# Expert rows added into one sum in DRAM by adding scatters, in a Macaron layer on one core

## The chip, the cores and the metric

The kernel runs on one core of one Trainium2 chip. The metric is the device time of one execution in microseconds (us); lower is better. TensorE (PE) multiplies matrices, VectorE (DVE) and ScalarE (ACT) work element by element and move results out of the matrix buffers (PSUM banks), GpSimd (POOL) does some element work and issues the indirect DMAs, and SyncE (SP) issues the plain ones.

## The reference

```python
x = L0_attn_inputs                                   # 4 x 256 tokens of 256, float32
x = x + 0.5 * ffn(layernorm(x))                      # mixture of experts
x = x + attention(layernorm(x))                      # 16 heads of 16, causal
x = x + 0.5 * ffn(layernorm(x))

def ffn(layer_input):
    logits = x @ router_weight.T                     # 8 experts
    top_vals, top_idx = jax.lax.top_k(logits, 2)
    gates = softmax(top_vals)
    for each expert e:                               # w_in 1024 x 256, w_out 256 x 512
        a, b = split(x @ w_in[e].T)
        acc = acc + gates[:, e] * (silu(a) * b @ w_out[e].T)
    return acc + bias
```

Each of the 1024 tokens takes part in two experts, so there are 2048 pairs of a token and an expert.

## The kernel before

**Blocks.** An expert phase (`ffn(0)` before the attention, `ffn(1)` behind it) is routed first: VectorE finds the two experts of each token, TensorE counts ranks by products, and the pairs, sorted by expert, are laid out in `BLOCKS` = 23 blocks of 128 slots. A block holds one expert's pairs; slots left over are empty. A one-hot product (L1264) finds which pair stands in each slot, and with it come `gather_row` and `scatter_row`.

**The loop over blocks.** For block j POOL gathers 128 normalised rows from `xn_scratch` (`gather`, L502). TensorE turns them (`turn_block`), multiplies them by both halves of w_in (`project`, three products for each since the float32 operands are split into a high and a low part), turns the gated middle (`turn_gated`) and multiplies by w_out (`combine`, L1311, again in three parts). In TensorE's order `combine(j)` stands between the turning and the projection of block j + 2. ScalarE makes the high parts, `silu` and the copy of the result out of PSUM (`copy_y`, L670); VectorE makes the low parts: `xT_lo`, `g`, `wo_lo` and `gT_lo`. In the first phase both also split each w_in (`split_high`, `split_low`) three blocks ahead. The first blocks are written out, the middle ones run in a hardware loop. The order of each engine is the order of the code; semaphores tie them together.

**Where the rows go.** For the first `SCATTERED` = 21 blocks `copy_y` writes ungated rows to one of two buffers `y`, and POOL scatters them (L510) to `y_scratch`, at the row of their pair, so no two scatters meet. At the phase's end SyncE waits for all scatters and loads both rows of each token (eight loads of 256 KB, L433). They are gated and added by VectorE (`add_rows`, L1010) or gated by ScalarE (`scale_rows`) and added up by TensorE through identity products (`add_scaled`, L1342). The rows of the last `LAST` = 2 blocks never leave the core: they are gated with `slot_gate` and spread over the tokens by one-hot products (`spread`, L1324) into four accumulators, one for each pair of token tiles; `settle` (L1022) adds an accumulator to x. Their gates are written to DRAM and gathered slot by slot (`gather_gates`, L526), and `zero_rows` (L516) scatters zeros to the pairs' places in `y_scratch`. The bias is added to x by POOL (`add_bias`, L496) after block 6. TensorE runs warming products on ones (`warm`) where it would stand still.

## Time and profile before

| | |
|---|---|
| Three runs | 436.99, 437.62, 437.9 us; median 437.62 us |
| Profiled execution | 439.45 us, its span from the first to the last instruction 437.4 us |
| Mean granted TensorE clock | 0.977 of full speed |
| Busy: PE, DVE, ACT, POOL | 408.1, 300.9, 256.8, 247.3 us |
| Scatters (L512) | 42, POOL busy 60.2 us |
| Gathers (L506) | 46, POOL busy 50.4 us |
| Loads of the scattered rows | 16 of 256 KB, landing 5.0 us after issue (median) |
| DMA traffic | 38.90 MB, 89 GB/s over the span |

"Busy" is the time in which an engine executes; the rest of the span it waits. A wait matters only where something on the way to the end waits with it; that way is what the chain of waits shows. Landing is counted from the start of the instruction that issues a DMA to the DMA's semaphore. The first expert phase lies at about 5 to 156 us of the span, the attention behind it, the second expert phase from about 295 us to the end.

### The profile page before, as it was taken

Reading aid. Unit: us, or ns where it says so; the run is one execution under the profiler, and the core shown is the slowest. Engines: PE = TensorE matmul, PEld = TensorE weight load, DVE = VectorE, ACT = ScalarE, POOL = GpSimd, SP = SyncE. Lnnn points to the kernel's source line nnn. Section 1 sums busy time; section 2 is a strip of 40 time slices with the busy share of each in tenths; the row PEclk is TensorE's granted clock in tenths of the full one; section 3 lists DMA queues with packets and bytes.
Section 4 is the critical chain, followed back from the end, with each engine's and each line's share of the span. In section 5 each row is a group of like instructions: output and inputs, shape, how many; then the busy total and the mean of one; then the engine's idle time right before and its main releaser. Section 6 shows DMA issues by size and latency. Waiting matters only on the chain.

```text
span 437.4 us, 10190 instructions
## 1 busy us (share of the span) xinstructions
PE 408.1 (93%) x2918; PEld 332.6 (76%) x2919; DVE 300.9 (69%) x613; ACT 256.8 (59%) x638; POOL 247.3 (57%) x307
## 2 busy tenths in 40 slices
PE   7878999999999989799999999898799999999995
PEld 3546888888888857588888888674488888888884
DVE  6768996865566697787677676866366575556565
ACT  2706885556655454788788787622255555655552
POOL 5136446866468359567777577200365586754860
PEclk9689999999999999999999999987999999999999
DMA  8729961111211620000000000007451112112136
GB/s 284 247 51 381 390 214 49 49 48 60 60 48 36 213 89 0 2 1 2 2 1 0 0 0 0 1 1 258 155 178 54 57 37 72 60 48 52 44 91 220
DMA packets 25738, 38.90 MB, mean 89 GB/s; under 512 B 3056, under 2 KB 20720, under 8 KB 25712
## 3 DMA queue, kind: packets, MB, share of 16 engines
q1 hardware_dynamic: 19088, 24.41, 16.3%
q0 software_dynamic: 4544, 12.07, 9.2%
q10 hardware_dynamic: 2080, 2.10, 1.4%
q8 instruction: 14, 0.23, 0.2%
q14 instruction: 12, 0.10, 0.1%
HBM read 29.37 MB, written 9.19 MB: 88 GB/s over the span
## 4 chain that ended last, share of the span: by engine, by line
PE 66%; DVE 13%; DMA 9%; issue 4%; ACT 3%; POOL 2%; SPq 1%; DVEq 0%; ACTq 0%; POOLq 0%
PE bank L1298 23%; PE bank L1320 12%; PE bank L1456 6%; PE bank L1221 4%; PE bank L1467 4%; PE bank L1308 3%; DMA w_out<-in_wout_t 3%; DMA w_out<-y_scratch 3%; PE bank L1423 2%; PE bank L1274 2%; PE bank L1503 2%; DMA arena<-xn_scratch,gather_row 1%; DMA y_scratch<-arena,scatter_row 1%; DVE arena L859 1%; PE bank L1457 1%
## 5 line engine op out<-in xcount | busy, mean ns | idle before, releaser
L506 POOL DMA_INDIRECT arena<-xn_scratch,gather_row x46 | 50.4, 1096 | 72.1 <-PE bank L1274 41.9
L512 POOL DMA_INDIRECT y_scratch<-arena,scatter_row x42 | 60.2, 1434 | 34.2 <-ACT arena L678 31.2
L987 DVE TENSOR_TENSOR wo_lo<-w_out,wo_hi 128x1024 fp32r<-128x1024 f32 x46 | 60.8, 1322 | 4.1 <-PE bank L1320 1.8
L1298 PE MATMUL bank<-w_hi,xT_hi 128*128 x184 | 62.4, 421 | 1.2 <-ACT xT_hi L637 1.2
L992 DVE TENSOR_TENSOR gT_lo<-bank,gT_hi 128x512 fp32r<-128x512 f32 x46 | 31.7, 690 | 39.3 <-ACT gT_hi L652 39.2
L1298 PE MATMUL bank<-w_hi,xT_lo 128*128 x184 | 58.0, 396 | 0.0
L1298 PE MATMUL bank<-w_lo,xT_hi 128*128 x184 | 57.6, 394 | 0.0
L590 POOL TENSOR_TENSOR k_head<-k_hi,head_mask 128x256 fp32r<-128x256 f32 x64 | 38.7, 625 | 28.1 <-PE bank L1457 21.0
L645 ACT ACTIVATE arena<-bank 128x512 f32<-128x512 f32 x46 | 27.5, 598 | 46.1 <-PE bank L1298 46.1
L667 ACT ACTIVATE wo_hi<-w_out 128x1024 fp32r x46 | 48.8, 1061 | 6.5 <-issue 4.1
L976 DVE TENSOR_TENSOR xT_lo<-bank,xT_hi 128x256 fp32r<-128x256 f32 x46 | 19.5, 424 | 37.3 <-ACT xT_hi L637 37.1
L1456 PE MATMUL bank<-k_head,xT_hi 128*128 128x256 f32 (+1 forms) x128 | 39.8, 392 | 1.9 <-ACT probs L775 1.2
L1298 PEld LDWEIGHTS bank<-w_lo,xT_hi 128*128 128x128 f32 x184 | 34.8, 189 | 8.2
L1298 PEld LDWEIGHTS bank<-w_hi,xT_lo 128*128 128x128 f32 x184 | 34.8, 189 | 8.0
L590 POOL TENSOR_TENSOR k_head<-k_lo,head_mask 128x256 fp32r<-128x256 f32 x64 | 38.3, 618 | 0.6 <-DVE k_lo L1102 0.6
L678 ACT ACTIVATE arena<-bank 128x256 f32<-128x256 f32 x42 | 16.2, 385 | 36.5 <-PE bank L1320 36.5
L1221 PE MATMUL bank<-ones 128*128 128x512 f16 x102 | 33.2, 480 | 2.8 <-POOL ident L459 1.8
L767 ACT ACTIVATE probs<-bank,neg_max 128x256 f32<-128x256 f32 x64 | 29.9, 478 | 8.7 <-DVE neg_max L1115 8.6
L1320 PE MATMUL bank<-wo_hi,gT_hi 128*128 128x256 f32 x184 | 33.0, 301 | 1.4 <-ACT gT_hi L652 1.4
L785 ACT ACTIVATE pT_hi<-bank 128x384 f16<-128x384 f32 x64 | 28.0, 488 | 10.4 <-PE bank L1467 9.9
L1128 DVE SCALAR_TENSOR_TENSOR pT_lo<-bank,pT_hi 128x384 f16<-128x384 f32 x64 | 32.4, 548 | 0.6
L1001 DVE TENSOR_TENSOR arena<-arena,bank 128x512 f32<-128x512 f32 x46 | 31.2, 678 | 0.9 <-issue 0.9
(180 smaller groups left out, 966.5 us busy)
## 6 DMA issues: line engine op xcount, KB each, us to landing
w_raw<-in_win_t SPq DMA_DIRECT2D x8, 1024.0 KB, 10.7
w_out<-in_wout_t SPq DMA_DIRECT2D x16, 512.0 KB, 8.3
w_out<-y_scratch SPq DMA_DIRECT2D x16, 256.0 KB, 5.0
xn_scratch<-arena ACTq DMA_DIRECT2D x2, 1024.0 KB, 6.3
x<-in_x SPq DMA_DIRECT2D x4, 256.0 KB, 3.5
out<-x SPq DMA_DIRECT2D x4, 256.0 KB, 2.1
arena<-xn_scratch,gather_row POOLq DMA_INDIRECT x46, 3.5
y_scratch<-arena,scatter_row POOLq DMA_INDIRECT x46, 3.0
```

The source lines that it names most:

```text
L506: pool.indirect_dma_start(out=xb[j % 2][:, :], out_offset=None, in_=xn_dram, in_offset=bass.IndirectOffsetOnAxis(ap=gather_row[:, j:j + 1] ...
L512: pool.indirect_dma_start(out=y_dram, in_=y[j % 2][:, :], in_offset=None, out_offset=bass.IndirectOffsetOnAxis(ap=scatter_row[:, j:j + 1], ...
L590: ins = pool.tensor_tensor(k_head[s % KSLOTS][:, part, hh, :], k[:, c, :].bitcast(F32), head_mask[:, h % HPC:h % HPC + 1].to_broadcast([P, ...
L667: act.activation(wo_hi[u][:, :, :], w_out[:, bass.ds(e, 1), :, :].rearrange("p o c d -> p (o c) d"), ACT.Copy)\
L987: dve.tensor_tensor(wo_lo[:, :, :], w_out[:, bass.ds(e, 1), :, :].rearrange("p o c d -> p (o c) d"), wo_hi[u][:, :, :].bitcast(F32), ALU.s ...
L992: dve.tensor_tensor(gT_lo[:, :, :], bank[4][:, :].rearrange("p (c t) -> p c t", c=HK), gT_hi[:, :, :].bitcast(F32), ALU.subtract).then_inc ...
L1001: dve.tensor_tensor(g[:, :], sa[:, :], bank[2 + u][:, :], ALU.mult).then_inc(g_done, 1)
L1128: dve.scalar_tensor_tensor(pT_lo[u][:, :, :], bank[3 + hh][:, 0:3 * P].rearrange("p (k t) -> p k t", k=3), P_SCALE, pT_hi[u][:, :, :], ALU ...
L1221: pe.matmul(bank[into][:, :], ones[:, :], bc(ones[:, :], 1, [P, 512 // P, P]), start=True, stop=True)
L1298: last = pe.matmul(bank[2 * half + u][:, :], tok[u][:, k, :], wts[:, bass.ds(e, 1), k, half * H:(half + 1) * H], start=(part == 0 and k == ...
L1320: last = pe.matmul(bank[y_bank(j)][:, 0:D], tok[:, c, :], wts[:, c, :], start=(part == 0 and c == 0), stop=(part == 2 and c == HK - 1))
L1456: pe.matmul(to, q[:, 1 if tail else 0, :], keys[:, part, :, 0:width], start=(n == 0), stop=False)
```

## The change

The scattered rows are gated first (`copy_y` scales by a column of `slot_gate`, now with a gate for each slot of all 23 blocks) and are scattered with an adding DMA into `sum_scratch`, one row for each token. The sum starts as a copy of x, written by SyncE (`start_sums`); at the end it is loaded straight into x, four loads of 256 KB. Two pairs of one token meet in one row, so each scatter waits for the one before it. Empty slots go to 128 spare rows behind the sum. The gates per slot come out of one-hot products: POOL computes the gates and splits them into three bf16 parts (`split_gates`), VectorE multiplies the block one-hots by them, TensorE multiplies 16 times by the row one-hots (69 columns), and VectorE sums the three parts. The bias enters the accumulators by a product of ones with a tile whose first three rows hold its three bf16 parts (`split_bias`, `spread_bias`). The zero scatters, the gates' way through DRAM, the additions of rows and the addition of the bias on POOL are gone. One w_in and one w_out are loaded before the first gathers rather than behind them, SyncE waits between the loads, and 11 rather than 18 warming products stand before the first phase's pair products.

```diff
-WARM_START, WARM_RANKS, WARM_PLAN, WARM_TURNED = 12, (18, 18), (6, 6), (4, 4)
+WARM_START, WARM_RANKS, WARM_PLAN, WARM_TURNED = 12, (11, 18), (6, 6), (4, 4)
@@ sync
+            def start_sums(f, first, tiles):
+                some = slice(first, first + tiles)
+                sp.dma_start(sum_rows[:, some, :], x[:, some, :]).then_inc(sum_started, 16)
-            load_w_in(0)
-            load_w_in(1)
-            load_w_in(2)
+            for e in range(EARLY):
+                load_w_in(e)
             load_w_out(0)
+            load_w_out(1)
+            load_w_in(EARLY)
             for parity in range(2):
                 sp.wait_ge(gathered[parity], 16)
-            for e in range(EARLY, E):
+            start_sums(0, 0, TILES)
+            load_w_out(2)
+            for e in range(EARLY + 1, E):
                 load_w_in(e)
-                load_w_out(e - EARLY + 1)
-            for e in range(E - EARLY + 1, E):
-                load_w_out(e)
+                load_w_out(e - 1)
+                sp.wait_ge(win_loaded[e - 1], 16)
+            load_w_out(E - 1)
...
+                    for b in range(BATCH):
+                        sp.wait_ge(attn_added, b + 2)
+                        start_sums(1, 2 * b, 2)
...
                 for i in range(TPAIRS):
-                    for k in range(TOPK):
-                        sp.dma_start(y_in[:, 2 * i:2 * i + 2, k, :], y_rows[:, k, 2 * i:2 * i + 2, :])\
-                            .then_inc(y_loaded[i], 16)
+                    sp.dma_start(x[:, 2 * i:2 * i + 2, :], sum_rows[:, 2 * i:2 * i + 2, :]).then_inc(y_loaded[i], 16)
@@ gpsimd
             def scatter(f, j):
                 pool.wait_ge(y_copied, f * SCATTERED + j + 1)
-                pool.indirect_dma_start(out=y_dram, in_=y[j % 2][:, :], in_offset=None,
-                                        out_offset=bass.IndirectOffsetOnAxis(ap=scatter_row[:, j:j + 1], axis=0))\
-                    .then_inc(scattered[j % 2], 16)
+                if j:
+                    pool.wait_ge(scattered[(j - 1) % 2], 16 * ((S_EVEN, S_ODD)[(j - 1) % 2] * f + (j + 1) // 2))
+                else:
+                    pool.wait_ge(scatter_ready, f + 1)
+                    pool.wait_ge(sum_started, 16 * (1 + BATCH * f))
+                pool.indirect_dma_start(out=sum_dram, in_=y[j % 2][:, :], in_offset=None,
+                                        out_offset=bass.IndirectOffsetOnAxis(ap=scatter_row[:, j:j + 1], axis=0),
+                                        compute_op=ALU.add).then_inc(scattered[j % 2], 16)
+            def split_gates(f):
+                ...
+                pool.wait_ge(e1_ready, f + 1)
+                then_gate(pool.tensor_scalar(den[:, :], e1[:, :], 1.0, None, ALU.add))
+                then_gate(pool.tensor_tensor(den[:, :], den[:, :], half_ones[:, 1, :], ALU.pow))
+                ...
@@ scalar
+                if isinstance(j, int) and j == 0:
+                    act.wait_ge(slot_gate_ready, f + 1)
+                column = slot_gate[:, j:j + 1] if isinstance(j, int) else slot_gate[:, bass.ds(j, 1)]
+                act.activation(y[u][:, :], bank[6][:, 0:D], ACT.Copy, scale=column).then_inc(y_copied, 1)
@@ vector
+            def mark_gates(f):
+                dve.wait_ge(gate_parts_ready, f + 1)
+                for part in range(PARTS):
+                    ins = dve.tensor_tensor(blk_gate[:, :, part, :], blk_hot[:, :, :],
+                                            bc(gate_part[:, part, :], 2, [P, PAIRS, BLOCKS]), ALU.mult)
+                ins.then_inc(gates_hot, 1)
+            def gather_gates(f):
+                dve.wait_ge(gates_done, f + 1)
+                parts = bank[7][:, 0:PARTS * BLOCKS].rearrange("p (a j) -> p j a", a=PARTS)
+                dve.tensor_reduce(slot_gate[:, :], parts, AX_X, ALU.add).then_inc(slot_gate_ready, 1)
@@ tensor
+            def spread_bias():
+                pe.wait_ge(bias_ready, 1)
+                for i in range(TPAIRS):
+                    pe.matmul(bank[ACC_BANK[i]][:, :], ones[:, :], bc(bias_rows[:, :], 1, [P, 2, D]), start=True, stop=False,
+                              skip_group_check=True)
...
+                    if not gated_next:
+                        spread_bias()
+                        spread(f, j - 1, range(1))
                     combine(f, j, u)
...
-                for j in range(SCATTERED, BLOCKS):
-                    spread(f, j)
-                add_scaled(f)
+                spread(f, SCATTERED, range(1, TPAIRS))
+                spread(f, SCATTERED + 1)
```

TensorE's order at the end of the second phase, from block 21's output product on, before (L1308 turns the gated middle, L1320 is the output product, L1334 the one-hot products):

```order
L1320 MATMUL bank<-wo_hi,gT_hi 128x256 x4
L1320 MATMUL bank<-wo_lo,gT_hi 128x256 x4
L1320 MATMUL bank<-wo_hi,gT_lo 128x256 x4
L1308 MATMUL bank<-ident,arena 128x128 x4
L1320 MATMUL bank<-wo_hi,gT_hi 128x256 x4
L1320 MATMUL bank<-wo_lo,gT_hi 128x256 x4
L1320 MATMUL bank<-wo_hi,gT_lo 128x256 x4
L1334 MATMUL bank<-gated_before,slot_hot 128x256 x16
L1334 MATMUL bank<-gated_last,slot_hot 128x256 x16
```

and after (L1319 is the output product, L1334 now the bias product, L1347 the one-hot products):

```order
L1319 MATMUL bank<-wo_hi,gT_hi 128x256 x4
L1319 MATMUL bank<-wo_lo,gT_hi 128x256 x4
L1319 MATMUL bank<-wo_hi,gT_lo 128x256 x4
L1307 MATMUL bank<-ident,arena 128x128 x4
L1334 MATMUL bank<-bias_rows,ones 128x512 x4
L1347 MATMUL bank<-gated_before,slot_hot 128x256 x4
L1319 MATMUL bank<-wo_hi,gT_hi 128x256 x4
L1319 MATMUL bank<-wo_lo,gT_hi 128x256 x4
L1319 MATMUL bank<-wo_hi,gT_lo 128x256 x4
L1347 MATMUL bank<-gated_before,slot_hot 128x256 x12
L1347 MATMUL bank<-gated_last,slot_hot 128x256 x16
```

The bias products and four of block 21's one-hot products now stand ahead of the last output product.

VectorE's order at the same place, before (L992 is gT_lo, L987 wo_lo, L1007 `gate_y_low`, L1018 `add_rows`, L1029 `settle`):

```order
L980 TENSOR_LOAD block_expert
L980 ISA x2
L992 TENSOR_TENSOR gT_lo<-bank,gT_hi 128x512
L1001 TENSOR_TENSOR arena<-arena,bank 128x512
L987 ISA
L987 TENSOR_TENSOR wo_lo<-w_out,wo_hi 128x1024
L992 TENSOR_TENSOR gT_lo<-bank,gT_hi 128x512
L1007 SCALAR_TENSOR_TENSOR gated_before<-bank,slot_gate,gated_before 128x256
L1018 SCALAR_TENSOR_TENSOR x<-w_out,gate,x 128x256 x2
L1007 SCALAR_TENSOR_TENSOR gated_last<-bank,slot_gate,gated_last 128x256
L1018 SCALAR_TENSOR_TENSOR x<-w_out,gate,x 128x256 x4
L1029 TENSOR_TENSOR x<-x,bank 128x512
```

and after (L1007 is now gT_lo, L1002 wo_lo, L1022 `gate_y_low`, L1030 `settle`):

```order
L995 TENSOR_LOAD block_expert
L995 ISA x2
L1007 TENSOR_TENSOR gT_lo<-bank,gT_hi 128x512
L1016 TENSOR_TENSOR arena<-arena,bank 128x512
L1002 ISA
L1002 TENSOR_TENSOR wo_lo<-w_out,wo_hi 128x1024
L1022 SCALAR_TENSOR_TENSOR gated_before<-bank,slot_gate,gated_before 128x256
L1007 TENSOR_TENSOR gT_lo<-bank,gT_hi 128x512
L1022 SCALAR_TENSOR_TENSOR gated_last<-bank,slot_gate,gated_last 128x256
L1030 TENSOR_TENSOR x<-x,bank 128x512 x4
```

`gate_y_low` of block 21 has moved ahead of gT_lo of block 22, and only the settlings are left behind the two.

VectorE's order at the first phase's first blocks, before (L873 splits w_in, L976 is xT_lo, L980 reads a block's expert, L1001 is g):

```order
L873 TENSOR_TENSOR w_lo<-w_raw,w_hi 128x1024 x2
L976 TENSOR_TENSOR xT_lo<-bank,xT_hi 128x256
L873 TENSOR_TENSOR w_lo<-w_raw,w_hi 128x1024 x2
L976 TENSOR_TENSOR xT_lo<-bank,xT_hi 128x256
L980 TENSOR_LOAD block_expert
L980 ISA x2
L1001 TENSOR_TENSOR arena<-arena,bank 128x512
L987 ISA
L987 TENSOR_TENSOR wo_lo<-w_out,wo_hi 128x1024
L873 TENSOR_TENSOR w_lo<-w_raw,w_hi 128x1024 x2
L980 TENSOR_LOAD block_expert
```

and after (L886 splits w_in, L991 is xT_lo, L977 `mark_gates`, L985 `gather_gates`):

```order
L886 TENSOR_TENSOR w_lo<-w_raw,w_hi 128x1024 x2
L991 TENSOR_TENSOR xT_lo<-bank,xT_hi 128x256
L886 TENSOR_TENSOR w_lo<-w_raw,w_hi 128x1024 x2
L991 TENSOR_TENSOR xT_lo<-bank,xT_hi 128x256
L977 TENSOR_TENSOR arena<-arena,gate_part 128x16x23 x3
L995 TENSOR_LOAD block_expert
L995 ISA x2
L1016 TENSOR_TENSOR arena<-arena,bank 128x512
L985 TENSOR_REDUCE slot_gate<-bank 128x23
L1002 ISA
L1002 TENSOR_TENSOR wo_lo<-w_out,wo_hi 128x1024
L886 TENSOR_TENSOR w_lo<-w_raw,w_hi 128x1024 x2
```

Three multiplications have come in ahead of the first g, and a reduction behind it.

## Rows read from the trace of the kernel before

**Rows 1.** Page, part 4: the chain that ended last, shares of the span by engine.

```profile
PE 66%; DVE 13%; DMA 9%; issue 4%; ACT 3%; POOL 2%; SPq 1%; DVEq 0%; ACTq 0%; POOLq 0%
```

**Rows 2.** Chain of waits, second phase's end: start us, us, what.

```profile
407.22 1.44 PE bank L1320 x12
...
412.08 1.45 PE bank L1320 x12
...
419.16 3.01 DMA y_scratch<-arena,scatter_row
...
425.71 6.16 DMA w_out<-y_scratch
...
434.12 0.69 DVE x L1029
```

**Rows 3.** Timeline, second phase's end: start, us, engine, line, operation, count [idle before <-releaser].

```profile
423.23 1.22 DVE L987 TENSOR_TENSOR wo_lo<-w_out,wo_hi 128x1024 fp32r<-128x1024 f32 x1 [0.92 <-PE bank L1320]
...
424.14 0.74 PE L1320 MATMUL bank<-wo_hi,gT_hi 128*128 128x256 f32 x4 [0.69 <-ACT gT_hi L652]
...
425.69 2.08 PE L1334 MATMUL bank<-gated_before,slot_hot 128*128 128x256 f32 x16
...
426.48 0.48 DVE L1007 SCALAR_TENSOR_TENSOR gated_last<-bank,slot_gate,gated_last 128x256 fp32r<-128x256 f32 x1
...
427.60 2.08 PE L1334 MATMUL bank<-gated_last,slot_hot 128*128 128x256 f32 x16
```

**Rows 4.** Timeline, first phase's end.

```profile
148.14 2.08 PE L1334 MATMUL bank<-gated_before,slot_hot 128*128 128x256 f32 x16
...
152.24 0.68 DVE L1029 TENSOR_TENSOR x<-x,bank 128x512 f32<-128x512 f32 x1
...
153.62 0.86 DVE L1018 SCALAR_TENSOR_TENSOR x<-w_out,gate,x 128x256 f32<-128x256 f32 x2
...
154.40 0.68 DVE L1029 TENSOR_TENSOR x<-x,bank 128x512 f32<-128x512 f32 x1
```

**Rows 5.** One line's instructions: scatters, all; scatter of 47.0; gathers of 321 to 409.

```profile
L512 POOL DMA_INDIRECT y_scratch<-arena,scatter_row x42: 980/1524/1968, 41.9 to 419.2; - x42
...
DMA to landing us min/median/max: 2.4/3.0/6.8
...
DMA to landing us min/median/max: 6.8/6.8/6.8
...
DMA to landing us min/median/max: 2.7/3.3/3.8
```

**Rows 6.** First phase's routing: chain row of the warming products, then VectorE's timeline.

```profile
16.74 6.43 PE bank L1221 x18
...
21.69 0.54 DVE L943 TENSOR_TENSOR arena<-arena,pair_id 128x368 f16<-128x368 f32 x1
...
23.60 0.18 DVE L952 TENSOR_SCALAR pair_i<-bank 128x23 int32<-128x23 f32 x1 [0.90 <-PE bank L1264]
```

**Rows 7.** VectorE's timeline, first blocks of the first phase.

```profile
34.29 0.42 DVE L976 TENSOR_TENSOR xT_lo<-bank,xT_hi 128x256 fp32r<-128x256 f32 x1 [2.79 <-ACT xT_hi L637]
35.29 0.69 DVE L1001 TENSOR_TENSOR arena<-arena,bank 128x512 f32<-128x512 f32 x1 [0.57 <-issue]
...
42.23 2.35 DVE L873 TENSOR_TENSOR w_lo<-w_raw,w_hi 128x1024 fp32r<-128x1024 f32 x2
44.51 0.68 DVE L992 TENSOR_TENSOR gT_lo<-bank,gT_hi 128x512 fp32r<-128x512 f32 x1
```

**Rows 8.** Timeline around POOL's addition of the bias in the first phase.

```profile
75.32 4.63 POOL L500 TENSOR_TENSOR x<-x,bias_half 128x2048 f32<-128x2048 f32 x1
...
77.04 3.99 DVE L987 TENSOR_TENSOR wo_lo<-w_out,wo_hi 128x1024 fp32r<-128x1024 f32 x1
...
76.18 0.64 PE L1320 MATMUL bank<-wo_hi,gT_lo 128*128 128x256 f32 x4
...
81.69 0.74 PE L1320 MATMUL bank<-wo_hi,gT_lo 128*128 128x256 f32 x4
```

More of the change, by code:

```diff
@@ L41 @@
 ACC_BANK = (7, 5, 3, 2)
[L43 to L44 removed]
 PAIRS = TOPK * TILES
 NEG = -1.0e30
+PARTS = 3
 AHEAD = 4
@@ L966, in route @@
[L966 to L970 removed]
+                then(dve.tensor_scalar(empty[:, :], pair_of, 0.0, trash_id[:, 0:1], ALU.is_equal, ALU.mult))
```

205 lines of the change are left out of this document (84 added, 121 removed).

## Prediction

> **What bounds the kernel now.** I read the page's chain by engine first, then the whole chain of waits in order of time, then the timeline of the two ends of the expert phases and of the start of the first, and last the landing times of the indirect DMAs. Two thirds of the chain are TensorE's own matmuls [rows 1]. In both expert phases the steady stage is TensorE's alone: the last product of one block starts 4.86 us after that of the block before (407.22, 412.08) [rows 2]. Whatever is done to scatters, bias or gates inside that stage is worth nothing as long as it fits into 4.87 us. The chain leaves TensorE at the stage's end: scatter 20 (3.01 us), eight loads of the scattered rows one after the other on SyncE, the last landing 6.16 us after its issue, and a last addition on VectorE at 434.12, which ends at 434.81; 2.6 us later the span ends [rows 2]. TensorE itself is through with the last one-hot products at 427.60 + 2.08 = 429.7 [rows 3], so some 5 us of the end are the way of the rows through DRAM. The first phase ends in the same way, but there VectorE's own work is the chain, with one addition of scattered rows (0.86 us) between two settlings [rows 4].
>
> **The end of the second phase.** After the change half the bytes are read back (four loads of 256 KB, straight into x), and the additions on VectorE, the scalings on ScalarE and the identity products on TensorE are gone. The last scatter starts at 419.2 as before; with 3.0 us of landing the four loads are issued from 422.2 on, each about 0.47 us, and should all be there by 427.5. What is late next is TensorE. The order there is new: bias product, block 21's products for pair 0, and only then the last block's output product. Pair 0's products need gate_y_low(21), which now stands right behind split_out_low(22) on VectorE: 423.23 + 1.22 = 424.45, + 0.48 = 424.9 [rows 3]. Four products at 1.91 / 16 = 0.12 us (the two groups of 16 start 1.91 us apart) end at 425.4; the last output product, which started at 424.14, starts 1.3 us later and, with 1.55 us as before (424.14 to 425.69), ends at 427.0. Then twelve products (1.43 us) and sixteen (1.91 us) give 430.35, and 0.1 for the handover, 430.5. The gating of block 22 (VectorE was through with it at 426.96, 1.3 us after the last output product) is hidden by the twelve. The four bias products stand in the wait for gate_y_low(21) and cost nothing; if that wait were gone, they would cost some 0.9 us. The settlings of pairs 0 to 2 lie under the products of the later pairs, the last one takes 0.69: 431.2 in place of 434.8. **-3.6 us.**
>
> **The end of the first phase** has the same pattern 277.55 us earlier (425.69 against 148.14). Pair 0 is complete there at 428.95 - 277.55 = 151.4 in place of 152.24, and the addition of 0.86 us between the first and the second settling goes, so that the second starts at about 152.75 in place of 154.40 [rows 4]. From there the chain is unchanged VectorE work. **-1.6 us.**
>
> **The adding scatter.** Each scatter now waits until the one before it has landed, and behind that wait on POOL stands the gather for the block five further on. Before, a scatter landed 2.4 to 3.0 us after its issue in the quiet stages, 0.98 to 1.6 us of which is POOL's own instruction; a gather landed after 2.7 to 3.8 [rows 5]. An adding scatter has to read its rows first, which no row shows. Bounds: 2.4 (as a plain one) and 3.0 + 2.6 = 5.6 (a whole gather's journey, its median 3.3 less about 0.7 of overlap, in series). I take 3.8, nearer to the scatter, since source and target rows can be read side by side. Under 4.8 it costs nothing in the steady stage. At the two ends a later landing is hidden too: pair 0 is needed at 428.95, so that the last scatter may take some 6.5 us. While the weights load, though, the scatter of 47.0 landed after 6.8 us [rows 5], more than a block (5.3 us there, below). With the new waits the first three or four scatters fall behind by 1.5 to 2 us each; gathers still come before TensorE needs them by my count, with little over. I put 0.4 us for it (0 to 5).
>
> *The Trainium skill* (DMA: Bandwidth & Descriptors, "Latency and other measured facts") gives 0.2 us on average for an access to HBM and 2 us under high load. Added to the plain scatter that is 3.2 or 5.0 us; by the second figure the steady stage would be slowed, by the first not. No row here decides between them.
>
> **The start of the first phase.** The one-hot pair products wait behind 18 warming matmuls that end at 23.17, while their operand is ready at 21.69 + 0.54 = 22.23 [rows 6]. With 11 of them (6.43 x 11 / 18 = 3.93 us from 16.74) TensorE is free at 20.7; the pair products then start at 22.3 and pair_i at about 22.85 in place of 23.60 (before it VectorE is busy till 22.7). **-0.75 us**, if the clock's dip behind it is no deeper than now. Against it stands the new gate work on VectorE: three multiplications of 128x368, each as the pair one (0.54, [rows 6]), between copy_xT_low(1) (ends 34.71) and the first g (35.29, [rows 7]): 1.62 us, of which the 0.58 us in which VectorE waits for its register load hide some; then a wait for 16 products on TensorE and a reduction, 0.2 to 0.3. For the next blocks VectorE is without a pause, since it splits the weights beside its usual work: 0.42 for xT_lo, 0.69 for g, 1.22 for wo_lo, 2.35 for w_lo and 0.68 for gT_lo are 5.3 us a block [rows 3, 7]. So it all arrives: **+1.3 us.** The loads are reordered, with 1.5 MB (one w_in, one w_out) brought forward and 1 MB of the residual written in between; as VectorE and not a load sets this stage, I count 0. The eight small gate steps on POOL run before the plan is there.
>
> **The bias.** The addition of the bias to all of x on POOL (4.63 us) held wo_lo on VectorE for 3.99 us in place of 1.22, and TensorE's third part of the output product came 5.51 us after the last one (76.18, 81.69) in place of 4.87 [rows 8]. It goes in both phases; in the second it cost nothing. **-0.6 us.** Its replacement, ten operations of 128x256 over three blocks in the first phase, fits between scatter and gather.
>
> **The second phase's start.** The 16 products of 69 columns for the gates stand on TensorE between block 1's halves, where little is waited for: at the price of those with 23 columns (23.17 to 23.60 with the handover, [rows 6]) or a bit over, +0.5. The gate multiplications on VectorE fall beside the first gather's descriptors, and the gate steps on POOL beside VectorE's routing, in which every step is on the path: +0.6 for both (0 to 2).
>
> The last price rests on [rows 8]: VectorE stood still for a POOL instruction. *The Trainium skill* (SBUF — State Buffer, "Who interferes with whom") says that a VectorE instruction with two SBUF inputs and a GpSimd one that reads SBUF exclude each other for the whole instruction. The trace agrees. By that rule a gate multiplication could hold the first gather for its 0.54 us and POOL's steps the routing for some 0.7 us in each phase, 1.9 us in place of my 0.6: 435.2.
>
> **Sum:** -3.6 - 1.6 + 0.4 - 0.75 + 1.3 - 0.6 + 0.5 + 0.6 = -3.75 us. The profiled execution had a span of 437.4 and took 439.45; it would take 435.7. The median of the runs is 437.62, 1.83 below it, so the forecast is 433.9.
>
> **Rivals.**
> *The chain of adds sets the pace (slower).* If an adding scatter lands later than about 4.8 us after its issue, each of some 20 scatters in a phase follows the last at landing + 0.1, and copy_y and through it TensorE wait for y. At 5.4, between the two bounds and near the upper, that is 0.63 x 20 x 2 = 25 us, less some 3 us at each end that the loads have to spare: 437.6 - 3.75 + 19 = 453. For it: the upper bound of [rows 5]; against it: 1.9 us between a plain scatter and the block's length.
> *It falls behind only while the weights load.* The scatters of the first four blocks land after 7 to 8.5 us, copy_y(3) waits, and 2 to 3 us are lost once: 436.0. For it: 6.8 us in [rows 5].
> *The hidden steps are not hidden (no change).* POOL's gate steps hold the routing twice for 1 to 1.5 us, the 1.62 us of multiplications hold the first gather, and the gate products start late: +3.5, 437.4. For it: [rows 8]; against: tiles of 8 and 16 columns.
> *More from the loads.* If, against my reading, loads brought forward shorten the first eight blocks by 0.3 us each, 2.4 us together: 431.5. Against it: VectorE's 5.3 us of such a block by themselves [rows 7].
>
> **How the numbers follow.** Forecast 0.52 (432.5 to 435.2), adds set the pace 0.18, behind under the loads 0.15, nothing hidden 0.07, more from the loads 0.08. A measurement here tells 0.2%, 0.9 us, from no change. Faster: 0.52 + 0.15 + 0.08 = 0.75; within it 0.07; slower 0.18. The range leaves out the most of the slower case and a sliver below: 430.8 to 441.0.
>
> **What would show it.** In the new profile: scatters landing under 4.8 us in the quiet stages and a POOL that waits for y_copied and not for scattered; blocks 4.87 us apart; the last output product starting 1.3 us later against its block's cadence; the last settling released by TensorE and not by a DMA, some 3.6 us earlier; pair_i at 22.8; the first g delayed. The forecast is wrong if the block period of the steady stage is above 4.9 us, or if the loads of x release the last settlings.

## The result: 7 to 8 us slower, and the profile after

The changed kernel takes 445.71 us (median of 4 runs, 444.52 to 445.9), the kernel before 437.76 beside it: a ratio over all runs of 1.0152, 95% interval 1.0121 to 1.0184. (The two medians lie 8.0 us apart, the ratio stands for 6.7 us.) The forecast was 433.9 us with a range to 441.0, so it had the wrong sign. The profiled execution took 445.52 us with a span of 443.8 (before 439.45 and 437.4), at granted clocks of 0.969 and 0.977. The two spans differ by 6.4 us; that is what the readings below divide up.

First the chain by engine and by line (part 4 of the page of after):

```profile
PE 53%; DMA 21%; DVE 11%; POOL 6%; issue 4%; ACT 4%; DVEq 0%; ACTq 0%; POOLq 0%
PE bank L1297 17%; DMA sum_scratch<-arena,scatter_row 15%; PE bank L1319 9%; PE bank L1461 6%; PE bank L1472 4%; DMA xn_scratch<-arena 3%; DMA arena<-xn_scratch,gather_row 3%; PE bank L1428 2%; PE bank L1220 2%; PE bank L1307 2%; PE bank L1508 2%; POOL sum_scratch L525 2%; ACT arena L694 2%; PE bank L1273 1%; PE bank L1462 1%
```

TensorE's share has gone from 66% [rows 1] to 53%, and the adding scatters hold 15%, where the plain ones had 1% of the chain before. To find where the time went I took the start of each block's output product (L1320 before, L1319 after) and subtracted. What a block "takes" is, below, the time from the start of the output product before it to that of its own.

| stretch (start of the output product of block ...) | before | after | added |
|---|---|---|---|
| first phase, 0 | 38.05 | 40.28 | +2.23 |
| 0 to 8 | 41.96 | 42.85 | +0.9 |
| 8 to 9 (bias addition gone) | 5.60 | 4.86 | -0.7 |
| 11 to 14 | 14.59 | 19.86 | +5.3 |
| 19 to 22 | 12.30 | 17.88 | +5.6 |
| 22 to the second phase's 0 | 172.77 | 168.17 | -4.6 |
| second phase, 0 to 21 | 102.07 | 102.07 | 0 |
| 21 to 22 | 2.71 | 4.48 | +1.8 |
| 22 to the end of the span | 13.2 | 9.2 | -4.0 |

So some 11 us are lost in two places of the first phase. The stretch 19 to 22 has three parts: 2.2 us at block 20, 1.6 at block 21, and 1.8 at block 22, which is the new order (the second phase's 21 to 22 has the same 1.8). The second phase's steady stage lost nothing: 4.87 us a block, as said. It has the same chain of adding scatters and the same one-hot rows on POOL at its end, but its first scatters land after 4.4 and 4.0 us and there is no bias to split; its blocks 19 and 20 take 4.86.

**How the first scatters go.** Chain of waits of after (start us, us, what):

```profile
44.24 9.05 DMA sum_scratch<-arena,scatter_row
...
53.34 0.73 issue
54.06 6.56 DMA sum_scratch<-arena,scatter_row
...
61.39 4.25 DMA sum_scratch<-arena,scatter_row
...
66.40 3.91 DMA sum_scratch<-arena,scatter_row
```

While weights load, two adding scatters land after 9.05 and 6.56 us, where a plain one of that stage had 6.8 [rows 5]. After that, from 75 us to the first phase's end, the landings are these (line L525 of after):

```profile
DMA to landing us min/median/max: 3.8/3.9/4.5
```

(The view is of 75 to 155 us.) The next scatter starts 0.77 us after a landing (44.24 + 9.05 = 53.29, and 54.06; I had 0.1). At its shortest the chain's period is 4.65 us (scatters 12 to 14, 115.81, 120.47 and 125.11), against a block of 4.87. But it doesn't work the backlog off at 0.2 us a block. Scatter 0 starts 4.0 us after its block's output product (44.24 against 40.28), scatter 2 9.6 us after it. In the loading stage, whose blocks are longer, that falls to 7.4 us at scatter 6, and there it stays: 7.6 at scatter 9 (95.57 against 87.99), 7.5 at 14, 7.6 at 17. From 6 to 9 and from 14 to 17 the scatters are 4.9 us apart, the same as the blocks, with landings of 3.9 to 4.5. The landing goes with the gather behind it on POOL: where that starts 1.9 us after the scatter, the landing is 3.75 to 3.9; where it starts 2.2 us after it or more, mostly 4.0 to 4.4. A gather waits for TensorE, so a chain that gets ahead meets longer landings. That this is what holds the backlog fits these times but was not tested.

**What the backlog does.** POOL's timeline of after, where the bias is made into rows:

```profile
95.57 1.87 POOL L525 DMA_INDIRECT sum_scratch<-arena,scatter_row  x1 [1.71 <-ACT arena L694]
96.92 1.46 POOL L555 TENSOR_SCALAR bias_half<-bias_half 128x256 f32<-128x256 f32 x1
98.45 0.40 POOL L557 CAST arena<-bias_half 128x256 bf16<-128x256 f32 x1
98.93 0.68 POOL L559 TENSOR_TENSOR arena<-bias_half,arena 128x256 f32<-128x256 f32 x1
99.69 1.64 POOL L561 TENSOR_TENSOR bias_rows<-arena,ident 128x256 bf16<-128x256 bf16 x1
101.60 1.05 POOL L513 DMA_INDIRECT arena<-xn_scratch,gather_row  x1 [0.27 <-POOL bias_rows L561]
102.95 1.62 POOL L525 DMA_INDIRECT sum_scratch<-arena,scatter_row  x1 [0.31 <-issue]
```

and TensorE's of the same time:

```profile
104.49 0.44 PE L1273 MATMUL bank<-ident,arena 128*128 128x128 f32 x2 [1.86 <-DMA arena<-xn_scratch,gather_row]
104.69 0.71 PE L1319 MATMUL bank<-wo_hi,gT_hi 128*128 128x256 f32 x4
```

The gather at 101.60 is block 14's, and TensorE turns block 14 ahead of block 12's output product. Since scatter 9 came at 95.57, four bias operations (with the scatter's own instruction they last from 95.57 to 101.33) push that gather beyond the need: TensorE stands for 1.86 us. It happens for three bias parts running (blocks 12, 13 and 14). The same happens at the end, where the one-hot rows for the last two blocks stand between scatter and gather:

```profile
139.82 1.82 POOL L525 DMA_INDIRECT sum_scratch<-arena,scatter_row  x1 [1.73 <-ACT arena L694]
141.12 2.91 POOL L574 TENSOR_SCALAR slot_hot<-col,slot_token 128x128 fp32r<-128x128 f32 x4
144.20 1.80 POOL L513 DMA_INDIRECT arena<-xn_scratch,gather_row  x1 [0.17 <-issue]
```

That gather is block 22's; it lands 4.55 us later, and block 20's output product waits for it until 148.98. What follows is the clock (TensorE's timeline, then a stretch of it with its granted clock behind the busy times):

```profile
148.79 0.44 PE L1273 MATMUL bank<-ident,arena 128*128 128x128 f32 x2 [1.96 <-DMA arena<-xn_scratch,gather_row]
149.50:153.00 3.50, 3.50 (x15) 3.12 (x14) 2.31 (x3) 0.62 (x2) 2.78 (x4) 0.53 0.03 5
```

After standing for 1.96 us TensorE is granted 0.53 of full speed (the lower of its two levels, 1.2 GHz, for nearly all of the stretch), and block 21 takes 6.28 us. In the profiles of *old order* and *gates early* below, block 20 waits as long (6.93 and 6.98), the clock stays whole, and block 21 takes 4.73. So the 1.6 us of block 21 are the clock's, and come or not after the same wait.

**The second phase's end** (timeline of after):

```profile
431.93 1.03 PE L1334 MATMUL bank<-bias_rows,ones 128*128 128x512 bf16 x4
...
433.52 1.90 SPq L439 DMA_DIRECT2D x<-sum_scratch  x4
...
433.98 0.72 PE L1347 MATMUL bank<-gated_before,slot_hot 128*128 128x256 f32 x4 [1.03 <-DVE gated_before L1022]
...
434.53 0.64 PE L1319 MATMUL bank<-wo_hi,gT_hi 128*128 128x256 f32 x4
...
437.41 2.08 PE L1347 MATMUL bank<-gated_last,slot_hot 128*128 128x256 f32 x16
...
438.19 2.48 DVE L1030 TENSOR_TENSOR x<-x,bank 128x512 f32<-128x512 f32 x4 [1.03 <-PE bank L1347]
```

It is the order that was forecast: bias products hidden in the wait, the last output product late, the loads of x done in time, the last settlings released by TensorE and not by a DMA as in [rows 2, 3].

### The profile page after: what moved, and what is told of

The parts are those of the page before. It is cut to its first block, busy times and chain, and to the rows that moved or that the text cites. A ratio compares the mean times of both kernels' runs of the same rounds, so it can differ in the third digit from the quotient of the medians.

```text
span 443.8 us, 10232 instructions
## 1 busy us (share of the span) xinstructions
PE 406.0 (91%) x2923; PEld 330.9 (75%) x2924; DVE 291.5 (66%) x587; ACT 255.3 (58%) x624; POOL 260.7 (59%) x321
## 3 DMA queue, kind: packets, MB, share of 16 engines
q0 software_dynamic: 8256, 11.54, 16.4%
## 4 chain that ended last, share of the span: by engine, by line
PE 53%; DMA 21%; DVE 11%; POOL 6%; issue 4%; ACT 4%; DVEq 0%; ACTq 0%; POOLq 0%
PE bank L1297 17%; DMA sum_scratch<-arena,scatter_row 15%; PE bank L1319 9%; PE bank L1461 6%; PE bank L1472 4%; DMA xn_scratch<-arena 3%; DMA arena<-xn_scratch,gather_row 3%; PE bank L1428 2%; PE bank L1220 2%; PE bank L1307 2%; PE bank L1508 2%; POOL sum_scratch L525 2%; ACT arena L694 2%; PE bank L1273 1%; PE bank L1462 1%
## 5 line engine op out<-in xcount | busy, mean ns | idle before, releaser
L525 POOL DMA_INDIRECT sum_scratch<-arena,scatter_row x42 | 74.9, 1784 | 59.6 <-ACT arena L694 44.8
L1297 PE MATMUL bank<-w_hi,xT_hi 128*128 x184 | 63.5, 427 | 1.3 <-ACT xT_hi L650 1.2
L1002 DVE TENSOR_TENSOR wo_lo<-w_out,wo_hi 128x1024 fp32r<-128x1024 f32 x46 | 57.4, 1247 | 5.4 <-PE bank L1319 4.0
L1007 DVE TENSOR_TENSOR gT_lo<-bank,gT_hi 128x512 fp32r<-128x512 f32 x46 | 31.7, 689 | 43.4 <-ACT gT_hi L665 43.4
L1297 PE MATMUL bank<-w_hi,xT_lo 128*128 x184 | 58.9, 402 | 0.0
L991 DVE TENSOR_TENSOR xT_lo<-bank,xT_hi 128x256 fp32r<-128x256 f32 x46 | 19.5, 424 | 47.3 <-ACT xT_hi L650 47.2
L694 ACT ACTIVATE arena<-bank,slot_gate 128x256 f32<-128x256 f32 x42 | 20.0, 475 | 46.1 <-PE bank L1319 25.2
L1220 PE MATMUL bank<-ones 128*128 128x512 f16 x95 | 30.8, 476 | 2.9 <-POOL ident L464 1.8
L1319 PE MATMUL bank<-wo_hi,gT_lo 128*128 128x256 f32 x184 | 31.0, 292 | 2.1 <-DVE gT_lo L1007 2.0
L1319 PE MATMUL bank<-wo_hi,gT_hi 128*128 128x256 f32 x184 | 32.8, 301 | 0.0
```

Source lines behind the costliest of these rows:

```text
L525: pool.indirect_dma_start(out=sum_dram, in_=y[j % 2][:, :], in_offset=None, out_offset=bass.IndirectOffsetOnAxis(ap=scatter_row[:, j:j + 1 ...
L1002: dve.tensor_tensor(wo_lo[:, :, :], w_out[:, bass.ds(e, 1), :, :].rearrange("p o c d -> p (o c) d"), wo_hi[u][:, :, :].bitcast(F32), ALU.s ...
L1007: dve.tensor_tensor(gT_lo[:, :, :], bank[4][:, :].rearrange("p (c t) -> p c t", c=HK), gT_hi[:, :, :].bitcast(F32), ALU.subtract).then_inc ...
L1220: pe.matmul(bank[into][:, :], ones[:, :], bc(ones[:, :], 1, [P, 512 // P, P]), start=True, stop=True)
L1297: last = pe.matmul(bank[2 * half + u][:, :], tok[u][:, k, :], wts[:, bass.ds(e, 1), k, half * H:(half + 1) * H], start=(part == 0 and k == ...
L1319: last = pe.matmul(bank[y_bank(j)][:, 0:D], tok[:, c, :], wts[:, c, :], start=(part == 0 and c == 0), stop=(part == 2 and c == HK - 1))
```

## The experiments

Twelve kernels in four groups, each group beside the kernel before on its chip (medians 439.35, 439.07, 439.51 and 439.04 us). My theory: scatters that wait for each other carry the loading stage's delay (the backlog) with them, and POOL's lumps of work, which such a delay leaves no room for, turn it into stalls of TensorE.

**No chain: two sums.** Scatters of odd blocks add into a second sum, which the result leaves out.

```diff
-                if j:
-                    pool.wait_ge(scattered[(j - 1) % 2], ...)
-                pool.indirect_dma_start(out=sum_dram, ...
+                pool.indirect_dma_start(out=(sum_dram, odd_dram)[j % 2], ...
```

> Changed kernel, but the scatters of odd blocks add into a second sum in DRAM and no scatter waits for the one before it any more (the second sum is left out of the output). Chain theory: the losses at blocks 12 to 14 (5.3 us) and 20 to 22 (4 us) of the first phase come only because each scatter waits for the last one's landing (3.9 to 4.2 us) and needs 0.7 us more to start, so that the backlog of the loading stage (9.1 and 6.6 us of landing) is never worked off. Both losses go: 445.7 - 9 = 436.5 us. Rival POOL's work: the bias split and the one-hot tiles are too much for POOL in a block whatever the scatters wait for; the losses stay, 445 us. Rival dear add: the adding DMA itself is slow; 444 to 445 us.

437.91 us, ratio 0.9979 (0.9951 to 1.0007), against 1.0152 for after: some 7.5 us come back with only the waits and the odd blocks' target changed. The landings are no shorter (3.7 to 4.5 us in the quiet stage). Blocks 12, 13 and 20 take 4.87, 4.88 and 4.86; only block 14 has 6.09. POOL's rows there:

```profile
104.56 2.30 POOL L523 DMA_INDIRECT odd_scratch<-arena,scatter_row  x1 [0.30 <-issue]
106.30 0.96 POOL L555 CAST arena<-arena 128x256 bf16<-128x256 f32 x1
107.35 0.61 POOL L561 TENSOR_TENSOR arena<-arena,ident 128x256 bf16<-128x256 bf16 x1
108.04 0.67 POOL L562 TENSOR_TENSOR bias_rows<-bias_rows,arena 128x256 bf16<-128x256 bf16 x1
109.50 1.66 POOL L514 DMA_INDIRECT arena<-xn_scratch,gather_row  x1 [0.79 <-POOL bias_rows L562]
111.46 1.60 POOL L523 DMA_INDIRECT sum_scratch<-arena,scatter_row  x1 [0.31 <-issue]
113.37 1.01 POOL L514 DMA_INDIRECT arena<-xn_scratch,gather_row  x1 [0.30 <-issue]
114.68 1.59 POOL L523 DMA_INDIRECT odd_scratch<-arena,scatter_row  x1 [0.30 <-issue]
```

Without a chain the bias work still makes one gather late (1.2 us), and POOL then catches up: scatters 3.2 us apart, which a chain of 4.65 cannot do. The result of this kernel is not that of the layer, since half of the sum is left out; it is there for its time alone, like the next.

**Plain scatters, waits kept** (`compute_op` taken out, so rows overwrite each other).

> Changed kernel with plain scatters in place of adding ones, every wait kept (the sum is left out of the computation, rows overwrite one another). Chain theory: a plain scatter lands after 3.0 us; with 0.7 us to start the next, 3.7 us a block is 1.2 us under the block's 4.87, so the backlog of the loading stage is gone some 6 blocks later, before the bias split of blocks 9 to 11 is done: about 437 us. Rival POOL's work: 445 us, since POOL does the same. Rival dear add: predicts about 437 us here as well, and is told apart by the two sums, whose scatters still add.

435.85 us, 0.992 (0.9888 to 0.9953). Landing 2.8 us; POOL catches up with scatters 3.2 us apart (106.77, 109.98, 113.19), and blocks 12 to 21 are all under 4.9. The wait at a plain scatter's landing costs nothing; it is wait and landing together. The kernel tells one thing more: with only the addition taken out of the scatters, the rest of the change brings 3.5 us, where my sum without the scatter's +0.4 had 4.15. The adding of the scatters alone is the distance from 0.992 to 1.0152, some 10 us.

**The kernel before with the wait.**

```diff
                 pool.wait_ge(y_copied, f * SCATTERED + j + 1)
+                if j:
+                    pool.wait_ge(scattered[(j - 1) % 2], ...)
```

> Kernel before, with one wait more: each scatter (plain, to its own rows as before) waits for the landing of the one before it. Chain theory: with a landing of 3.0 us and 0.7 us to start the next the chain is 3.7 us a block, under 4.87, so the backlog of the loading stage (6.8 us landings) is worked off and nothing reaches TensorE but for at most 1 us at the bias addition: 0 to +1 us against the kernel before. Rival (waiting itself is dear, whatever the landing): +5 us or more.

439.37 us, 1.0008 (0.997 to 1.0045). It agrees from the other side: in its profile the scatters fall behind under the loads and are level with the blocks again at block 6.

**The bias in nine pieces**, one or two operations in each of blocks 8 to 16 instead of three or four in 9 to 11.

```diff
-                    if f == 0 and E < j <= E + PARTS:
-                        split_bias(j - E - 1)
+                    if f == 0 and E <= j < E + 9:
+                        split_bias(j - E)
```

> Changed kernel with the same bias split in nine pieces of one or two POOL operations, one piece a block from block 8 on, in place of three pieces of 3 to 5 us. Chain theory: scatter, gather and a piece of up to 1.3 us fit under the landing of 3.9 us, so the 5.3 us at blocks 12 to 14 go, the backlog and with it the 4 us at blocks 20 to 22 stay: 440.5 us. Rival POOL's work: POOL has the same work in all, so at most the peak is spread and 1 to 2 us are gained: 444 us.

441.6 us, 1.0044 (1.0011 to 1.0077): 4.7 us below after's ratio. Blocks 12 to 14 take 4.86. But 17, 19 and 20 now take 5.57, 5.86 and 5.42, together 2.3 us too long, where after lost 2.2 at block 20 (and 1.6 at 21 by the clock): the backlog stays at 7.6 us and meets the next lumps.

**A gather further ahead** (`AHEAD` 5 in place of 4).

> Changed kernel with gathers issued five blocks ahead in POOL's order rather than four, so that the gather a late scatter held up stands one scatter further forward. Chain theory: TensorE waited at blocks 12 to 14 and 20 to 22 for gathers that stood behind a waiting scatter; with a block's length more of cover most of the 9 us go, unless the copy of y, which waits for the scatter two blocks back, becomes the wait instead: 438 to 441 us. Rival POOL's work: POOL is full in those blocks, the order changes nothing: 445 us.

445.85 us, 1.019 (1.0123 to 1.0257): a miss for me. I had taken the gather for the only thing that the backlog makes late. The group of `copy_y`, which needs its buffer's scatter to have landed (page of this kernel):

```profile
L694 ACT ACTIVATE arena<-bank,slot_gate 128x256 f32<-128x256 f32 x42 | 20.0, 476 | 60.6 <-DMA sum_scratch<-arena,scatter_row 56.3
```

With gathers early, ScalarE waits for landings (56.3 us in all), and blocks 3 to 5 take 6.15, 5.79 and 5.68, blocks 13 to 15 5.91, 6.73 and 5.97. Two y buffers allow a lag of two blocks at most; what the gather no longer stops, they stop. Blocks 19 to 21 are free of loss (4.86, 4.86, 4.74), so the backlog reaches the phase's end, and there it costs too. In the second phase scatter 20 starts at 429.4, where after has 429.8 for a last product that comes 3.7 us later, and the settlings wait for the loads of x behind it:

```profile
436.38 1.43 DVE L1030 TENSOR_TENSOR x<-x,bank 128x512 f32<-128x512 f32 x2 [2.91 <-DMA x<-sum_scratch]
438.40 1.39 DVE L1030 TENSOR_TENSOR x<-x,bank 128x512 f32<-128x512 f32 x2 [0.59 <-DMA x<-sum_scratch]
```

From block 22's product to the end it takes 11.57 us, after 9.23.

**Old order of the weight loads**, and **gates before the second xT_lo**.

```diff
             for e in range(EARLY):
                 load_w_in(e)
             load_w_out(0)
-            load_w_out(1)
-            load_w_in(EARLY)
...
             start_sums(0, 0, TILES)
+            load_w_in(EARLY)
+            load_w_out(1)
```

> Changed kernel with the loads of the fourth w_in and the second w_out issued behind the first gathers again, as before the change. If the first gather is late (25.1 in place of 24.0 us) because the store of the normalised rows landed after 13.0 us in place of 8.2 behind those loads, the gather starts at about 24.1 and 1 us is won: 445 on a chip where the changed kernel takes 446. Rival: the loads are then late for blocks 1 and 2 and the backlog of the scatters grows: 0 or slower.

> Changed kernel with VectorE's three gate multiplications of the first phase moved ahead of xT_lo of block 1, into the 3.2 us in which VectorE waited for it. If they delayed the first g by about 1.3 us and all behind it, block 0's output product comes 1.3 us earlier and, as everything to block 11 is VectorE's or TensorE's chain, 1 to 1.3 us are won at the end: 444.8 on a chip where the changed kernel takes 446. Rival: scatters set the pace from block 3 on, so an earlier start only waits longer: no change.

444.76 us, 1.0128 (1.0089 to 1.0167), and 444.18, 1.0133 (1.0086 to 1.0179). Both lie some 1 us under after's 1.0152, and both intervals reach it: inconclusive by time. The profile of the old order does show what it was for: the store of xn lands after 9.3 us in place of 13.0, and the first gather starts at 23.58 in place of 25.11.

**All three edits together.**

> The bias split in nine pieces, the loads behind the gathers and the gate multiplications early, together in the changed kernel. Chain theory: -4.4 (pieces, as measured), -1 and -1.3, so about 439.3 us where the kernel before takes 439.4: the loss is taken back but the gain of both ends is spent on the backlog at blocks 17 to 20 and on the later last output product. If the parts do not add up (scatters set the pace): 441 us.

440.33 us, 1.0026 (1.0006 to 1.0045): the best whole version of the change, still not below the kernel before. POOL's rows at the late blocks:

```profile
132.97 1.61 POOL L525 DMA_INDIRECT sum_scratch<-arena,scatter_row  x1 [0.30 <-issue]
134.04 2.91 POOL L575 TENSOR_SCALAR slot_hot<-col,slot_token 128x128 fp32r<-128x128 f32 x4
137.13 1.07 POOL L513 DMA_INDIRECT arena<-xn_scratch,gather_row  x1 [0.18 <-issue]
138.51 1.84 POOL L525 DMA_INDIRECT sum_scratch<-arena,scatter_row  x1 [0.30 <-issue]
```

The gather at 137.13 is block 22's, and block 20 takes 5.32. Block 21's starts at 131.65, behind the two operations of the last bias piece (128.94 to 130.87), and block 19 takes 6.01: the pieces are smaller lumps, but still lumps.

**Two sums made whole.** The second sum starts from zeros, and VectorE adds it to x before the settlings; the three edits above are in.

```diff
+                sp.dma_start(odd_rows, bias_half[:, :]...)
...
                     sp.dma_start(x[:, 2 * i:2 * i + 2, :], sum_rows[...])
+                    sp.dma_start(y_in[:, 2 * i:2 * i + 2, :], odd_rows[...])
```

> A whole kernel: scatters of odd blocks add into a second sum that starts from zeros, no scatter waits for the one just before it, the two sums are added on VectorE before the last settlings (four additions of 128x512, about 0.6 each), the bias is split in nine pieces over nine blocks, weights load in the old order, gates before the second xT_lo. Two megabytes more move while weights load and at the attention stage, and each tail reads one more megabyte. Theory (the chain of adding scatters and the lumps on GpSimd are the whole loss behind the first block): the version with two sums left 437.9 with 1.2 us at block 14, which the pieces take away, and the gates 0.4: 436.3, plus at most 1 for the zeros among the weight loads and 1 at the first tail: 436.3 to 438.3, ratio 0.993 to 0.998, blocks 12 to 21 of the first phase all at 4.9 us. Rival (the adding scatter costs by its traffic whatever it waits for): the larger traffic of this version makes it 439 to 441, with weight-load blocks above 5.4 us.

452.38 us, 1.0308 (1.0282 to 1.0334). The theory's part held, blocks 7 to 21 of the first phase take 4.74 to 4.88, but what I had priced at 2 us cost far more. Its chain of waits:

```profile
32.12 9.92 DMA w_out<-in_wout_t
...
155.05 5.87 DMA w_out<-odd_scratch
...
160.94 0.07 DVE x L1054
```

One more megabyte among the weights: block 1 takes 11.04 us in place of 5.99. (The kernel before with the wait had 11.04 there too in its profile and no loss in its median, so how much of it is the zeros stays open.) And each tail has eight loads in place of four, the last landing 5.87 us after its issue: the first settling starts at 161.5, 9.7 us after block 22's output product at 151.85, where after has 3.7 (163.47 against 159.81). The gain of the tail is gone with the second sum.

**The scatter ahead of the gather** in POOL's order, on the version with the three edits.

```diff
+                    scatter(f, j)
                     if j + AHEAD < BLOCKS:
                         gather(f, j + AHEAD)
-                    scatter(f, j)
```

> The version with bias pieces, old loads and early gates (1.0026), and on GpSimd each scatter ahead of the gather of four blocks on, instead of behind it. If part of the chain is that a scatter whose turn has come stands behind a gather that waits for TensorE, the chain loses that part and the late blocks 17 to 20 go to 4.9: 0.996 to 0.999. Rival: the gather now stands behind the scatter's wait for the landing, which costs more slack than it gives: 1.003 to 1.01, with gathers as the releaser of TensorE.

443.18 us, 1.0103 (1.0076 to 1.0129): the rival. POOL's timeline:

```profile
42.00 2.11 POOL L525 DMA_INDIRECT sum_scratch<-arena,scatter_row  x1 [9.62 <-ACT arena L695]
44.42 1.32 POOL L513 DMA_INDIRECT arena<-xn_scratch,gather_row  x1 [0.30 <-PE bank L1273]
50.86 1.59 POOL L525 DMA_INDIRECT sum_scratch<-arena,scatter_row  x1 [5.12 <-DMA sum_scratch<-arena,scatter_row]
...
103.21 1.60 POOL L525 DMA_INDIRECT sum_scratch<-arena,scatter_row  x1 [1.24 <-ACT arena L695]
```

The gathers now stand behind the waits, and blocks 1 to 4 take 7.63, 7.42, 7.28 and 6.41, 5.9 us more than in the version it is built on. That is the backlog paid at once; afterwards scatter 10 comes 3.1 us after its block's product (98.34, 95.22), released by ScalarE and not by a landing, and blocks 6 to 18 take 4.9. But paying early doesn't free the late blocks: 19 and 20 take 5.81 and 5.60, and in the second phase, which has no backlog, blocks 20 and 21 take 7.17 and 6.29, where every other kernel here has 4.9 and 4.7. There the gather of block 22 starts at 418.75, behind the one-hot rows and a scatter, and TensorE stands 2.08 us for it; then its clock is granted at 0.57 from 425 to 429 us. So in this order the one-hot rows alone are enough for a stall, which the chain theory doesn't cover.

**Parts of the change in the kernel before.** First only the warm-up of 11 products, then with the bias by product in nine pieces as well.

```diff
-WARM_START, WARM_RANKS, ... = 12, (18, 18), ...
+WARM_START, WARM_RANKS, ... = 12, (11, 18), ...
```

> The kernel before with the first warm-up cut from 18 to 11 products, nothing else. If the term of my sum was right, pair_i comes 0.75 us earlier and the first gather with it: 438.3 where the kernel before has 439.1, ratio 0.998. Rival: the first gather then waits for the store of xn instead, or the lower clock takes it back: ratio 1.000.

> The kernel before with two of the change's parts and nothing else of it: the first warm-up of 11 products, and the bias as three rows of a product, its rows made in nine pieces over blocks 8 to 16 instead of the addition to x on GpSimd. The warm-up alone had 0.9979 of the kernel before. If the bias term was right (its addition made block 9 of the first phase 0.74 us long, and the products hide under block 22), that block goes to 4.87 and the whole to 0.996, 437.7 where before has 439.5. Rival: the pieces between plain scatters delay a gather as they did between adding ones: a block of 12 to 20 above 4.9, and 0.998 or more.

438.47 us, 0.9979 (0.9961 to 0.9997), and 438.0, 0.9988 (0.9968 to 1.0007). In the first the first gather starts at 24.13 in place of 24.87. In the second block 9 is level with the others (TensorE's timeline):

```profile
79.68 0.72 PE L1339 MATMUL bank<-wo_hi,gT_hi 128*128 128x256 f32 x4
...
84.54 0.72 PE L1339 MATMUL bank<-wo_hi,gT_hi 128*128 128x256 f32 x4
```

4.86 us where before has 5.60, and blocks 10 to 20 stay at 4.9. The time doesn't show it: the interval is wider than 0.74 us, and its lower end, 0.9968, stays above the 0.996 expected. In its profile blocks 1 to 8 take 0.7 us more than before, which takes the gain back; why isn't known. The only kernel with the right result here that beats the one before is the plain warm-up cut, by 0.2%.

## Why the prediction was wrong

**The step that failed** is that of the adding scatter: "Under 4.8 it costs nothing", with "+0.4" for the loading stage, and in the rival "landing + 0.1". The landing was mis-sized by little (3.9 for 3.8). The handover was 0.77, and I had counted the loading stage's delay as one that ends with the stage ("lost once", in the rival). It was 9.05 + 6.56 us of landing, and of the 9.6 us by which the scatters were behind, 7.6 were still there at the phase's late blocks. A threshold on the period says that a chain doesn't slow the steady stage, and that held; it says nothing of what is left for the next disturbance. Nor did "gathers still come before TensorE needs them" hold: they stand behind the late scatter on POOL, and TensorE waited 1.86 and 1.96 us for them. In place of +0.4 the adding cost some 10 us (plain scatters 0.992, adding ones 1.0152), and some 7.5 of them go with the waits (two sums 0.9979).

**And the bias:** "fits between scatter and gather". I had set ten operations (there are eleven) against POOL's idle time, and not against the gather that is queued behind them: as it stands in the program, three or four operations with a scatter already late. With adding scatters and no chain they cost 1.2 us (two sums), with plain scatters and a chain nothing (blocks 12 to 21 of that run); with both the three parts cost 5.3. The gain of the removed addition was right, 0.74 for 0.6. The one-hot rows at blocks 19 to 22 I didn't price at all; they had been there before, and are there in the second phase, with no backlog and at no cost.

The two rivals closest to this each had half: *it falls behind only while the weights load* had the cause but took the loss as ending there; *the chain of adds sets the pace* had the sign and the wrong place: no steady stage slowed, and in it the scatters kept the blocks' 4.87.

**What held.** The order of the second phase's end, and TensorE as its last releaser. The last settling ends at 440.67; less the 8.62 by which that phase was late, 432.05 for the forecast 431.2: -2.8 of -3.6, since block 22's product came 1.8 later and not 1.3, and the last addition ended 1.2 us after the last product, not 0.8. The stores of the output then took back 0.5 us, so the span's end gained 2.2.

At the first phase's end this profile gained 2.75 us from block 22's product on, of which its delay took 1.8: -0.9 for -1.6. That is a lucky profile. From that product to the first `k_head` of the attention it took 14.1 us, before 16.8; but 16.0, 16.0, 17.5 and 17.7 in four runs with the same code there (gates early, all three edits, old order, nine pieces). In those TensorE is granted 0.79, 0.79, 0.62 and 0.62 of its clock somewhere in an 8 us stretch between 156 and 172 us, in after and in the kernel before it has the whole of it there. With the later product such a run has no gain at this end.

The second phase's start cost 0.5 us for 1.1: the gate products made the way from the first gather to the first output product 11.79 us long in place of 11.26, as priced. The steps before that gather cost nothing: from the last `pT_lo` of the attention to it, two runs of the changed kind (gates early, all three) take 22.89 us, and the kernel before with the bias by product takes 22.88. Of the 0.6 us of my sum, or the 1.9 of the rival price behind it, nothing shows on this way. (Of the table's -4.6 us, the other 2.4 lie there: before took 25.32 for that way, after 22.93. Its clock was granted at 0.60 from 294 to 298 us and after's was whole; that is no part of the change.)

**The start** went half as forecast. pair_i came at 22.78 (22.85 forecast), but the gather waits for something else (POOL's timeline of after):

```profile
25.11 1.89 POOL L513 DMA_INDIRECT arena<-xn_scratch,gather_row  x1 [2.91 <-DMA xn_scratch<-arena]
```

The store of xn was issued at 11.24 and landed 13.0 us later (8.2 before), behind the loads brought forward; with the old order it landed after 9.3, and in the four profiles with that order the first gather starts at 23.4 to 23.6, in the six with the new one at 24.1 to 25.3. In the kernel before the same warm-up cut did bring the gather forward by the 0.74 us forecast. "I count 0" for the reordered loads was so an error too, of at least the size of that gain. Then g comes late as said: its start is at 37.54, behind 1.44 us of gate work (VectorE, after):

```profile
35.84 0.42 DVE L991 TENSOR_TENSOR xT_lo<-bank,xT_hi 128x256 fp32r<-128x256 f32 x1 [3.19 <-ACT xT_hi L650]
36.18 1.44 DVE L977 TENSOR_TENSOR arena<-arena,gate_part 128x368 bf16<-128x368 f32 x3
37.54 0.68 DVE L1016 TENSOR_TENSOR arena<-arena,bank 128x512 f32<-128x512 f32 x1
```

The start's +2.23 us goes with the clock. TensorE is granted half of it from 24 to 32 us and 0.79 from 32 to 36 in after; before has 1.00, 0.57 and 1.00 in 24 to 28, 28 to 32 and 32 to 36. The first output product comes at 40.2 to 40.5 us in the three profiles that are so slow there (after, nine pieces, two sums), and at 37.5 to 38.4 in three of the changed kind whose clock fell for as short as before's 38.05 (further ahead, gates early, plain). The prediction had set as a condition that the clock's dip be no deeper than before; in this profile it was. With 11 warming products TensorE does less ahead of it, but in three of the changed kind the dip stayed short, so that this is its cause isn't shown.

What stays open: why the chain doesn't work off its backlog in the steady stage, with 4.65 us at its shortest against 4.87; how often the clock falls after a stall or at the first phase's end, and how much of the medians' distance that is; and whether a third y buffer, with a gather further ahead, would gain anything, since the run with the gather further ahead shows that the backlog has a price at the phase's end as well. It wasn't tried.

## What to carry to other kernels

When a change makes transfers wait for each other, work out the chain's period with its handover, subtract it from the stage's, and ask how many rounds that slack needs at best to pay off the worst transfer before it. Then look in a profile whether the lag really falls: here it stood at 7.6 us where the slack promised 0.2 a block. If it doesn't fall, the delay is there for good and every lump of work queued on the issuing engine must be held against it. Operations put "into idle time" of an engine that also issues DMAs are priced by the DMA behind them, not by their sum. And a fix that only removes one releaser is to be checked for the next: here the gather, then the y buffer, then the lumps.

## What the runs showed of the hardware

- An adding scatter of 128 rows of 1 KB landed after 3.9 us (median of the quiet stage), with the same waits as a plain one at 2.8. Under loads two took 9.05 and 6.56, two plain ones with the same waits 6.88 and 6.66.
- It makes more packets: the software queue, which carries the gathers too, had 8256 for 11.54 MB with adding scatters and 4224 for the same bytes with plain ones, with 16.4% and 8.8% of the DMA engines' time. POOL's own instruction takes 1.78 us on average, not 1.43 as in the kernel before.
- From a scatter's landing to the start of the next one, which waited for it, 0.77 us passed (53.29 to 54.06).
- Two waits of TensorE of 1.86 and 1.96 us were each followed by a stretch at little over half of full speed (0.57 from 105 to 109 us, 0.53 from 149.5 to 153); in two other profiles a wait as long was followed by none.
